# Graph attention on one Trainium2 core: messages and index copy moved within the slot of TensorE and VectorE

## The chip, the cores and the metric

The kernel runs on one core of one Trainium2 chip. The metric is device time in microseconds (us) of one execution. Three timed runs of the kernel before took 2605.95, 2622.97 and 2636.16 us; the median is 2622.97 us.

## What is computed

A graph of 1250 nodes with 768 features each and 41,250 directed edges goes through two layers of GATv2 attention, a linear-attention block and a feed-forward block. Only the attention layer matters here:

```
def gatv2_layer(x, Ws, bs, Wd, bd, attn, src, dst):
    hs = (x @ Ws + bs).reshape(N, H, HD)
    hd = (x @ Wd + bd).reshape(N, H, HD)
    hs_e = hs[src]
    e = jax.nn.leaky_relu(hs_e + hd[dst], SLOPE)
    logits = jnp.einsum('ehd,hd->eh', e, attn)
    m = jax.ops.segment_max(logits, dst, num_segments=N)
    ex = jnp.exp(logits - m[dst])
    s = jax.ops.segment_sum(ex, dst, num_segments=N)
    alpha = ex / s[dst]
    out = jax.ops.segment_sum(alpha[..., None] * hs_e, dst, num_segments=N)
    return jax.nn.elu(out).reshape(N, DM)
```

N is 1250, H is 8 heads of 96 features, and there are two such layers. The edges are sorted by destination.

## The kernel before

Before `attend` runs, `hs` of all nodes lies in HBM as `table` (1280 rows of 800 floats, 1250 of them nodes) and `hd` lies in SBUF as `dst_rows`. `attend` then walks over the edges in macros of 4 tiles of 128 edges (`G` = 4), 91 macros in each layer (`NM` = 91), 182 in both.

One macro goes through three steps, which belong to three different slots of the loop:

1. Turn. GpSimd has gathered the macro's 512 rows of `table` into `rows[b]` with four indirect DMAs of 128 rows (`gather`, L475 to L484), each by a column of `index[b]`. TensorE adds the destination's row and the gathered row in PSUM and turns them so that features lie on partitions (`turn_chunk`, L552): six chunks of 128 features, each with four pairs of matmuls (L559 and L561, one pair for each tile). ScalarE takes each chunk through a Relu into `at_relu` (`bend`, L502).
2. Head. VectorE joins the chunks of two pairs (`join`, L653). TensorE sums over the features of each head (`sum_heads`, L574 and L578, four tiles of 8 columns side by side). VectorE runs a scan from the left and one from the right for the segment maximum (`scan_left` L659, `scan_right` L664), subtracts it (`shift`, L668), TensorE turns the result back (`turn_back`, L584), ScalarE takes the exponential (`weights`, L512), and VectorE multiplies it into a one-hot matrix (`spread_out`, L676).
3. Message. TensorE multiplies this matrix with the gathered rows (`messages`, L597, 32 matmuls of which the trace shows two passes each, 64 in all; each uses 32 columns of the array). VectorE adds the totals to `sums` (`add_total`, L686, 8 instructions). After that the gathered rows are no longer needed, and VectorE copies the indices of the macro four later into the same buffer (`copy_index`, L696).

A slot works on three macros at once: head of h, message of h-1, turn of h+1. The engines run one slot function each, and the order inside it is written by hand. On TensorE (L601) it is: load of the block numbers (`places_of`), messages, chunk 0, heads, chunks 1 to 3, turn back, chunk 4, drops, linear part, chunk 5. On VectorE (L698): line up, join, additions, index copy, both scans, shift, first maximum, place, linear, spread. The four buffers of `rows`, `index` and `place` go round by macro number (`UNROLL` = 4).

The waits around the change are semaphores. GpSimd waits for `index_ready` before the four gathers of a macro; its third gather also waits for the counter `scanned` of three macros earlier to be complete (this counter's last step is `first_maximum`), and its fourth for `spread_ready`. Chunk 0 waits for `gathered[b]`, all 64 increments of the macro's four gathers, and for `place_ready`. The sending of the gathers, in its own words:

```
def gather(m, b, paced=True):
    pool.wait_ge(index_ready, m + 1)
    for j in range(G):
        if paced and j == 2:
            pool.wait_ge(scanned, (m - 3) * SCANS + 2 * SCANS)
        if paced and j == 3:
            pool.wait_ge(spread_ready, m - 2)
        pool.sem_inc(index_seen, 1)
        pool.indirect_dma_start(rows[b][:, j, :], None, table, ...)
```

So the macro whose index is copied in the slot of head h is h+3, and its chunk 0 stands in the slot of head h+2: two slots later.

## Time and profile before

| | |
|---|---|
| median of three runs | 2622.97 us |
| span of the profiled execution, first to last instruction | 2250.3 us |
| difference, outside the span | 372.7 us |
| busy share of the span: TensorE, VectorE, ScalarE, GpSimd | 96%, 75%, 50%, 40% |
| granted TensorE clock, mean | 0.986 |

The profile holds one execution, whose own time outside the span is not listed; the span is what the sums below are made against, and what lies around it (372.7 us against the median) is taken to stay. The two attention layers fill the stretches from about 539 to 1222 us and from about 1430 to 2120 us of the span, 61% of it. In a timeline row the columns are: start (us), duration (us), engine, line, operation, what is written and read, count; in brackets the idle time before it and what ended it. Merged rows give the time from the first start to the last end.

### The profile page before, as it was taken

Reading aid. Unit: us, or ns where it says so; the run is one execution under the profiler, and the core shown is the slowest. Engines: PE = TensorE matmul, PEld = TensorE weight load, DVE = VectorE, ACT = ScalarE, POOL = GpSimd, SP = SyncE. Lnnn points to the kernel's source line nnn. Section 1 sums busy time; section 2 is a strip of 40 time slices with the busy share of each in tenths; the row PEclk is TensorE's granted clock in tenths of the full one; section 3 lists DMA queues with packets and bytes.
Section 4 is the critical chain, followed back from the end, with each engine's and each line's share of the span. In section 5 each row is a group of like instructions: output and inputs, shape, how many; then the busy total and the mean of one; then the engine's idle time right before and its main releaser. Section 6 shows DMA issues by size and latency. Waiting matters only on the chain. (4 is left out here: it accounts for less than half of the span.)

```text
span 2250.3 us, 86767 instructions
## 1 busy us (share of the span) xinstructions
PE 2154.9 (96%) x31007; PEld 1684.2 (75%) x31007; DVE 1678.2 (75%) x4435; ACT 1133.4 (50%) x2749; POOL 896.5 (40%) x849
## 2 busy tenths in 40 slices
PE   8999999998999999999997999899999999999798
PEld 4665555555888888888886655688888888888676
DVE  5546872344888888888887755588888888888884
ACT  1101200034666666666664314566666666666584
POOL 0000001022666566666652211466656656656121
PEclk9999999999999999999998999999999999999899
DMA  5002044144777777787774024587777777777421
GB/s 192 1 0 71 20 142 133 57 131 133 249 250 247 249 250 243 248 252 239 247 245 153 29 97 132 168 252 242 251 242 248 240 245 250 244 246 238 171 88 48
DMA packets 143398, 404.07 MB, mean 180 GB/s; under 512 B 21811, under 2 KB 81625, under 8 KB 143073
## 3 DMA queue, kind: packets, MB, share of 16 engines
q0 software_dynamic: 59584, 298.64, 41.0%
q1 hardware_dynamic: 79691, 93.00, 13.8%
q10 hardware_dynamic: 3828, 7.85, 1.0%
q8 instruction: 264, 4.33, 0.8%
q14 instruction: 31, 0.25, 0.0%
HBM read 370.77 MB, written 17.17 MB: 172 GB/s over the span
## 5 line engine op out<-in xcount | busy, mean ns | idle before, releaser
L502 ACT ACTIVATE at_relu<-at_turned,ah_attn_size 128x512 f32<-128x512 f32 x1092 | 716.2, 692 | 392.0 <-PE at_heads L578 363.4
L483 POOL DMA_INDIRECT at_rows<-table,ah_index x360 | 404.6, 1124 | 269.0 <-DVE ah_index L696 158.5
L483 POOL DMA_INDIRECT ah_room<-table,ah_index x352 | 399.8, 1136 | 260.8 <-DVE ah_index L696 174.3
L561 PE MATMUL at_turned<-ident,ah_room 128*128 128x128 f32 x2208 | 427.9, 280 | 2.3 <-issue 2.3
L559 PE MATMUL at_turned<-ah_place,dst_rows 96*128 96x128 bf16 x2208 | 407.7, 223 | 23.4 <-ACTq L537 19.2
L561 PE MATMUL at_turned<-ident,at_rows 128*128 128x128 f32 x2160 | 413.3, 277 | 1.7 <-issue 1.4
L559 PE MATMUL at_turned<-at_place,dst_rows 96*128 96x128 bf16 x2160 | 394.1, 222 | 2.2 <-issue 1.5
L686 DVE SCALAR_TENSOR_TENSOR sums<-sums,at_factor,at_total 128x97 f32 x1456 | 343.7, 310 | 1.4 <-DVE at_gap L751 0.7
L561 PEld LDWEIGHTS at_turned<-ident,ah_room 128*128 128x128 f32 x2208 | 318.1, 144 | 26.2 <-issue 1.7
L561 PEld LDWEIGHTS at_turned<-ident,at_rows 128*128 128x128 f32 x2160 | 307.8, 143 | 24.5 <-issue 2.2
L676 DVE TENSOR_TENSOR at_spread<-at_lined,at_weight 128x1024 f32<-128x1024 f32 x182 | 223.3, 1227 | 127.7 <-ACT at_weight L512 127.7
L559 PEld LDWEIGHTS at_turned<-ah_place,dst_rows 96*128 x2208 | 224.1, 103 | 60.6 <-issue 60.5
L653 DVE SCALAR_TENSOR_TENSOR at_relu<-at_relu,ah_pair_sign 128x512 f32<-128x512 f32 x364 | 256.3, 746 | 0.0
L559 PEld LDWEIGHTS at_turned<-at_place,dst_rows 96*128 x2160 | 217.4, 103 | 36.8 <-issue 36.6
L597 PE MATMUL at_total<-at_rows,at_spread 128*32 128x100 f32 x5760 | 144.3, 253 | 1.9 <-DVE at_spread L676 1.8
L597 PE MATMUL at_total<-ah_room,at_spread 128*32 128x100 f32 x5888 | 145.7, 251 | 0.3 <-issue 0.2
L597 PEld LDWEIGHTS at_total<-ah_room,at_spread 128*32 128x32 f32 x5888 | 125.6, 110 | 12.3 <-DVE at_spread L676 2.4
L597 PEld LDWEIGHTS at_total<-at_rows,at_spread 128*32 128x32 f32 x5760 | 124.5, 111 | 13.2 <-DVE at_spread L676 3.9
L518 ACT ACTIVATE at_factor<-at_back,first_dst 128x2 f32<-128x2 f32 x728 | 132.8, 283 | 1.1 <-PE at_back L589 1.1
L578 PE MATMUL at_heads<-at_relu,ah_sign_mask 128*8 128x128 f32 x2912 | 116.5, 273 | 1.6 <-issue 1.4
L574 PE MATMUL at_heads<-at_relu,ah_sign_mask 128*8 128x128 f32 x2912 | 114.0, 273 | 0.2 <-issue 0.2
L1748 ACT ACTIVATE pr_parts<-pr_dst_row 128x384 bf16<-128x384 f32 x60 | 31.2, 522 | 124.9 <-DVEq L1845 112.0
(317 smaller groups left out, 3179.7 us busy)
## 6 DMA issues: line engine op xcount, KB each, us to landing
at_flags<-run_flags SPq DMA_DIRECT2D x182, 64.0 KB
dst_rows<-pr_parts SPq DMA_DIRECT2D x76, 144.0 KB, 2.6
ah_place<-local_rows SPq DMA_DIRECT2D x92, 96.0 KB
at_place<-local_rows SPq DMA_DIRECT2D x90, 96.0 KB
table<-ah_room SPq DMA_DIRECT2D x20, 400.0 KB, 2.4
ah_room<-table,ah_index POOLq DMA_INDIRECT x368
at_rows<-table,ah_index POOLq DMA_INDIRECT x360
mx_w<-in_L_mix_W_qkv SPq DMA_DIRECT2D x4, 1152.0 KB, 11.8
```

The costliest lines, as they stand in the source:

```text
L483: pool.indirect_dma_start(rows[b][:, j, :], None, table, bass.IndirectOffsetOnAxis(index[b][:, j:j + 1], 0)).then_inc(gathered[b], 16)
L502: act.activation(relu[c][:], turned[chunk(b, c)][:], ACT.Relu, scale=attn_size[:, c:c + 1]).then_inc(bent, 1)
L518: act.activation(factor[b % 2][:, j, :], back[:, P + j * HH:P + (j + 1) * HH], ACT.Exp, scale=first_dst[:, bass.ds(m * G + j, 1)]).then_in ...
L559: pe.matmul(into, dst_rows[0:SP_ROWS, bass.ds(at[j], 1), c * P:(c + 1) * P].rearrange("p o d -> p (o d)"), place[b][:, j * P:(j + 1) * P], ...
L561: last = pe.matmul(into, rows[b][:, j, c * P:(c + 1) * P], ident[:], is_transpose=True, start=False, stop=True)
L574: pe.matmul(head_row(j), sign_mask[:, c, :], relu[c][:, j * P:(j + 1) * P], start=False, stop=False)
L578: last = pe.matmul(head_row(j), sign_mask[:, c, :], relu[c][:, j * P:(j + 1) * P], start=False, stop=c == JOINED[-1][1])
L597: last = pe.matmul(part(j)[h % HM * S:(h % HM + 1) * S, h // HM, :], spread[:, j, h, :], rows[b][:, j, :].rearrange("p (g h r) -> p h g r" ...
L653: dve.scalar_tensor_tensor(relu[c][:], relu[from_][:], pair_sign[:, c:c + 1], relu[c][:], ALU.mult, ALU.add).then_inc(joined, 1)
L676: dve.tensor_tensor(spread[:], lined[:].unsqueeze(2).broadcast_to([P, G, H, S]), weight[:].rearrange("p (j h) -> p j h", j=G).unsqueeze(3) ...
L686: dve.scalar_tensor_tensor(into[:, k], into[:, k], factor[b % 2][:, j, k:k + 1], part(j)[:, k, 0:HW], ALU.mult, ALU.add).then_inc(added, 1)
L1748: act.activation(heads_half(parts[t % 2][:, s, :], half), heads_half(dst_row[:], half), ACT.Copy).then_inc(split_done, 1)
```

## The change

TensorE's slot now begins with chunks 0 and 1, then sums the heads, then does the messages; chunk 2, the turn back, and chunks 3 and 4 follow. The block numbers of the next slot are loaded (`blocks(coming)`) after the messages of this one, in place of a load at the slot's start. VectorE builds the place matrix and the linear part right behind the joins, runs the scans and the shift, then waits for the messages (`totalled`), copies the index, and only then does the eight additions, the first maximum and the spread. Nothing is added to or taken from the arithmetic.

```
--- before.py
+++ after.py
@@ -598,39 +598,42 @@
                                              rows[b][:, j, :].rearrange("p (g h r) -> p h g r", h=H, r=QUAD)[:, h], start=True, stop=True)
                     last.then_inc(totalled, 1)
 
-                def slot(turn, head, message):
+                def blocks(turn):
+                    return places_of(nc, mybir.EngineType.PE, block_of, turn[0], 1) if turn else None
+
+                def slot(turn, head, message, at, coming):
                     if turn:
-                        at = places_of(nc, mybir.EngineType.PE, block_of, turn[0], 1)
+                        turn_chunk(*turn, at, 0)
+                        turn_chunk(*turn, at, 1)
+                    if head:
+                        sum_heads(head[0], head[1])
                     if message:
                         for pair in range(2):
                             messages(message[0], message[1], pair)
+                    after = blocks(coming)
                     if turn:
-                        turn_chunk(*turn, at, 0)
-                    if head:
-                        sum_heads(head[0], head[1])
-                    if turn:
-                        for c in range(1, 4):
-                            turn_chunk(*turn, at, c)
+                        turn_chunk(*turn, at, 2)
                     if head:
                         turn_back(head[0])
                     if turn:
+                        turn_chunk(*turn, at, 3)
                         turn_chunk(*turn, at, 4)
                     if head:
                         sum_drops(head[0])
                     if turn:
                         turn_linear(turn[0])
                         turn_chunk(*turn, at, 5)
+                    return after
 
                 pe.sem_inc(weights_ready, EXPS)
                 pe.sem_inc(added, ADDS)
-                slot(macro(0, 0), None, None)
-                slot(macro(0, 1), macro(0, 0), None)
-                for i in range(LOOPS):
-                    for b in range(UNROLL):
-                        slot(macro(i, b + 2), macro(i, b + 1), macro(i, b))
-                slot(macro(LOOPS, 2), macro(LOOPS, 1), macro(LOOPS, 0))
-                slot(None, macro(LOOPS, 2), macro(LOOPS, 1))
-                slot(None, None, macro(LOOPS, 2))
+                at = blocks(macro(0, 0))
+                at = slot(macro(0, 0), None, None, at, macro(0, 1))
+                at = slot(macro(0, 1), macro(0, 0), None, at, macro(0, 2))
+                for m in range(2, NM):
+                    at = slot(macro(0, m), macro(0, m - 1), macro(0, m - 2), at, macro(0, m + 1) if m + 1 < NM else None)
+                slot(None, macro(0, NM - 1), macro(0, NM - 2), None, None)
+                slot(None, None, macro(0, NM - 1), None, None)
                 pe.wait_ge(merge_ready, 1)
                 pe.wait_ge(weights_ready, NM * EXPS + EXPS)
                 pe.matmul(back[:, 0:2 * G * HH], head_rows[:], gap[:].rearrange("p s k -> p (s k)"), start=True, stop=True).then_inc(merged, 1)
@@ -701,21 +704,22 @@
                     if head:
                         line_up(head[0], fresh)
                         join(head[0])
-                    if message:
-                        for j in range(G):
-                            add_total(message[0], message[1], j, at)
-                    if more:
-                        copy_index(message[0] + UNROLL, message[1])
-                    if head:
-                        scan_left(*head)
-                        scan_right(head[0], head[1])
-                        shift(head[0])
-                        first_maximum(head[0])
                     if after:
                         build_place(*after)
                     if turn:
                         line_linear(*turn, head is None)
                     if head:
+                        scan_left(*head)
+                        scan_right(head[0], head[1])
+                        shift(head[0])
+                    if more:
+                        dve.wait_ge(totalled, message[0] * 2 + 2)
+                        copy_index(message[0] + UNROLL, message[1])
+                    if message:
+                        for j in range(G):
+                            add_total(message[0], message[1], j, at)
+                    if head:
+                        first_maximum(head[0])
                         spread_out(head[0], head[1])
 
                 dve.memset(linear[:], 0.0).then_inc(cleared, 1)
```

TensorE before, around the start of a steady slot in the first layer (at_turned are the chunks' PSUM banks, at_total the messages', ISA rows compute an address from the block number):

```order
L559 MATMUL at_turned_0<-ah_place,dst_rows 128x128
L561 MATMUL at_turned_0<-ident,ah_room 128x128
L370 TENSOR_LOAD block_of
L597 MATMUL at_total_0<-ah_room,at_spread 32x100 x32
L559 ISA
L559 MATMUL at_turned_0<-at_place_0,dst_rows 128x128
L561 MATMUL at_turned_0<-ident,at_rows_0 128x128
L559 ISA
```

and around the head sums of the same slot (at_heads):

```order
L559 MATMUL at_turned_0<-at_place_0,dst_rows 128x128
L561 MATMUL at_turned_0<-ident,at_rows_0 128x128
L574 MATMUL at_heads<-at_relu_0,ah_sign_mask 8x128 x8
L578 MATMUL at_heads<-at_relu_0,ah_sign_mask 8x128 x8
L559 ISA
L559 MATMUL at_turned_0<-at_place_0,dst_rows 128x128
```

TensorE after, the end of chunk 1 and what follows:

```order
L559 ISA
L559 MATMUL at_turned_0<-at_place_0,dst_rows 128x128
L561 MATMUL at_turned_0<-ident,at_rows_0 128x128
L574 MATMUL at_heads<-at_relu_0,ah_sign_mask 8x128 x8
L578 MATMUL at_heads<-at_relu_0,ah_sign_mask 8x128 x8
L597 MATMUL at_total_0<-ah_room,at_spread 32x100 x32
L370 TENSOR_LOAD block_of
L559 ISA
L559 MATMUL at_turned_0<-at_place_0,dst_rows 128x128
L561 MATMUL at_turned_0<-ident,at_rows_0 128x128
```

The head sums and the messages stand next to each other, the load of block numbers has moved behind them, and the messages no longer come first.

VectorE before, in the loop of the second layer, the last additions of a slot and what follows (sums are the totals, at_left and at_right the two scans):

```order
L686 ISA
L686 SCALAR_TENSOR_TENSOR sums<-sums,at_factor_1,at_total_1 128x97
L686 ISA
L686 SCALAR_TENSOR_TENSOR sums<-sums,at_factor_1,at_total_1 128x97
L696 ISA
L696 COPY ah_index<-src_index 128x4
L659 SCALAR_TENSOR_TENSOR at_left_1<-at_flags_1,at_left_1,at_heads 128x128
L663 REGISTER_ALU
L664 SCALAR_TENSOR_TENSOR at_right<-at_flags_1,at_left_1 128x128
L667 REGISTER_ALU
L668 TENSOR_TENSOR at_shifted<-at_heads,at_right 128x128
```

VectorE after, from the left scan on (L716 is the new wait's instruction):

```order
L662 SCALAR_TENSOR_TENSOR at_left_1<-at_flags_1,at_left_1,at_heads 128x128
L666 REGISTER_ALU
L667 SCALAR_TENSOR_TENSOR at_right<-at_flags_1,at_left_1 128x128
L670 REGISTER_ALU
L671 TENSOR_TENSOR at_shifted<-at_heads,at_right 128x128
L716 ISA
L699 ISA
L699 COPY ah_index<-src_index 128x4
L683 REGISTER_ALU
L685 REGISTER_ALU
L686 ISA
L689 ISA
```

The index copy stood behind the additions and ahead of the scans; now both scans and the shift stand ahead of it, and the additions behind it.

## Rows read from the trace of the kernel before

**Rows 1.** The page: TensorE's busy time, and DMA's busy tenths in 40 slices

```profile
PE 2154.9 (96%) x31007; PEld 1684.2 (75%) x31007; DVE 1678.2 (75%) x4435; ACT 1133.4 (50%) x2749; POOL 896.5 (40%) x849
...
DMA  5002044144777777787774024587777777777421
```

**Rows 2.** Windows, a steady stretch: busy us of each engine, clock, DMA share, GB/s

```profile
700.00:900.00 200.00, 199.02 (x4061) 174.53 (x4049) 175.65 (x516) 135.38 (x357) 122.71 (x110) 1.00 0.78 248
```

**Rows 3.** Waits, whole span: engine, line, what it waited for, total us, times, longest

```profile
ACT at_relu L502 <- PE at_heads L578: 363.4, 180, 3.1
...
POOL ah_room L483 <- DVE ah_index L696: 174.3, 88, 7.7
...
DVE at_spread L676 <- ACT at_weight L512: 127.7, 182, 2.1
```

**Rows 4.** Timeline of TensorE, one slot of the first layer: start, us, engine, line

```profile
861.82 0.28 PE L561 MATMUL at_turned<-ident,at_rows 128*128 128x128 f32 x1
...
862.03 1.58 PE L597 MATMUL at_total<-at_rows,at_spread 128*32 128x100 f32 x64
...
863.54 0.23 PE L559 MATMUL at_turned<-ah_place,dst_rows 96*128 96x128 bf16 x1
...
864.13 0.28 PE L561 MATMUL at_turned<-ident,ah_room 128*128 128x128 f32 x1
...
864.34 0.62 PE L574 MATMUL at_heads<-at_relu,ah_sign_mask 128*8 128x128 f32 x16
...
864.78 0.62 PE L578 MATMUL at_heads<-at_relu,ah_sign_mask 128*8 128x128 f32 x16
...
865.33 0.23 PE L559 MATMUL at_turned<-ah_place,dst_rows 96*128 96x128 bf16 x1
...
865.92 0.28 PE L561 MATMUL at_turned<-ident,ah_room 128*128 128x128 f32 x1
...
866.04 0.22 PE L559 MATMUL at_turned<-ah_place,dst_rows 96*128 96x128 bf16 x1
```

**Rows 5.** Timeline of TensorE at the first layer's end, where heads follow messages

```profile
1209.48 1.58 PE L597 MATMUL at_total<-ah_room,at_spread 128*32 128x100 f32 x64
...
1210.88 0.62 PE L574 MATMUL at_heads<-at_relu,ah_sign_mask 128*8 128x128 f32 x16
```

**Rows 6.** Timeline of VectorE: the spreads that bound the layer, and one slot

```profile
551.29 1.23 DVE L676 TENSOR_TENSOR at_spread<-at_lined,at_weight 128x1024 f32<-128x1024 f32 x1 [1.08 <-ACT at_weight L512]
...
860.69 1.23 DVE L676 TENSOR_TENSOR at_spread<-at_lined,at_weight 128x1024 f32<-128x1024 f32 x1 [0.65 <-ACT at_weight L512]
...
863.60 1.89 DVE L686 SCALAR_TENSOR_TENSOR sums<-sums,at_factor,at_total 128x97 f32 x8
865.40 0.17 DVE L696 COPY ah_index<-src_index 128x4 int32 x1
865.47 0.48 DVE L659 TENSOR_TENSOR_SCAN at_left<-at_flags,at_left,at_heads 128x128 f32<-128x128 bf16 x1
...
867.97 1.23 DVE L676 TENSOR_TENSOR at_spread<-at_lined,at_weight 128x1024 f32<-128x1024 f32 x1 [0.67 <-ACT at_weight L512]
...
1208.20 1.23 DVE L676 TENSOR_TENSOR at_spread<-at_lined,at_weight 128x1024 f32<-128x1024 f32 x1 [1.07 <-ACT at_weight L512]
```

**Rows 7.** Timeline of GpSimd: first and last gather of the macro indexed at 865.40

```profile
866.36 0.95 POOL L483 DMA_INDIRECT at_rows<-table,ah_index  x1 [1.86 <-DVE ah_index L696]
...
870.32 1.44 POOL L483 DMA_INDIRECT at_rows<-table,ah_index  x1 [0.30 <-issue]
```

**Rows 8.** Timeline of TensorE: chunk 0 of that same macro

```profile
878.18 0.23 PE L559 MATMUL at_turned<-at_place,dst_rows 96*128 96x128 bf16 x1
```

**Rows 9.** Timeline of GpSimd, the first layer's last macro of gathers

```profile
1191.78 0.94 POOL L483 DMA_INDIRECT at_rows<-table,ah_index  x1 [1.85 <-DVE ah_index L696]
...
1195.93 1.45 POOL L483 DMA_INDIRECT at_rows<-table,ah_index  x1 [0.30 <-issue]
```

**Rows 10.** Windows behind it: columns as in rows 2, DMA share and GB/s last

```profile
1199.00:1200.00 1.00, 1.00 (x14) 0.93 (x13) 0.97 (x5) 1.00 (x3) 0.00 (x0) 1.00 0.44 122
1200.00:1201.00 1.00, 1.00 (x14) 0.94 (x12) 0.25 (x3) 0.67 (x4) 0.00 (x0) 1.00 0.15 55
1201.00:1202.00 1.00, 1.00 (x14) 0.95 (x12) 1.00 (x1) 1.00 (x3) 0.00 (x0) 1.00 0.00 0
```

## The prediction, made before the changed kernel ran

> **What bounds the kernel now.** I read the page first. TensorE is busy 96% of the span, and in the attention layers every slice of the DMA row stands at 7 tenths [rows 1]. The windows view of a steady stretch says it more sharply: of 200 us TensorE is busy 199.02, VectorE 175.65, ScalarE 135.38, and the 16 DMA engines 0.78 of the time at 248 GB/s; the clock is granted in full [rows 2]. So TensorE's order of work sets the slot, and nobody waits long for anybody: the reader is to see in the waits that ScalarE waits for the heads (363.4 us), GpSimd for indices (174.3 us) and VectorE for the weights (127.7 us over 182 slots, 0.70 each), which cost nothing while TensorE is full [rows 3].
>
> The period of a quiet slot is the distance of two spreads, 867.97 - 860.69 = 7.28 us. Over the first layer it is (1208.20 - 551.29) / 89 = 7.38 us [rows 6]; the 0.10 between are odd stalls. There are 180 such steps in two layers, 1,330 us of the span.
>
> TensorE is busy, but not dense. A full-width matmul group followed by another starts 0.16 us before the nominal end of the one ahead: 865.92 + 0.28 against 866.04. Where it changes from full width to narrow columns or back, the next starts only 0.07 before the end: 861.82 + 0.28 against 862.03 (chunk to messages), 863.61 against 863.54 (messages to chunk), 864.13 + 0.28 against 864.34 (chunk to heads), 865.40 against 865.33 (heads to chunk) [rows 4]. Messages and heads are both narrow, and at the layer's end, where heads follow messages, they start 0.18 before the end (1211.06 against 1210.88) [rows 5]. So each change of width costs about 0.10 us, and a slot has four of them. The page "TensorEngine Tiling (Array Packing)" of the Trainium skill, section Key Properties, gives the mechanism: a change of tiling mode drains TensorE, a change of tile within a mode does not. By that rule alone the change would be faster.
>
> **The change on TensorE.** The orders show chunk, heads, messages, chunk. Two changes of width go (chunk to messages, heads to chunk), and in their place come chunk 5 to chunk 0 and heads to messages, neither of them a change of width. That takes off 2 x 0.10 = 0.20 us: a quiet slot would be 7.08 us. All matmuls stay. The load of block numbers moves behind the messages; the trace's rows do not count such instructions, so I bound it: nothing if TensorE has enough queued, and at most the 0.35 us of idle time that would show in front of chunk 2 if all of it came bare. That end is my estimate from the whole gain and a little more; behind 64 narrow matmuls (1.58 us [rows 4]), which the sequencer can hand over ahead of time, I take 0.
>
> **The change on VectorE and ScalarE.** The scans come as soon as the heads are there, as before (865.40 to 865.47, [rows 4, 6]), so ScalarE gets its work at the same point. The additions (1.80 us, 863.60 to 865.40) move behind the shift, into the 0.70 us of waiting for the weights and beyond it. VectorE's work stays at 175.65 / 200 x 7.28 = 6.39 us of a slot [rows 2], under 7.08. I cost both at 0.
>
> **The change on GpSimd's gathers.** This is the step that decides. GpSimd can gather macro h+3 only when VectorE has copied its index, and TensorE wants its rows in chunk 0, two slots later. Both ends of this lead move against each other. Let T be the end of the heads of slot h.
>
> Before: the index is copied at T (865.40, where the heads end at 864.78 + 0.62), the first gather issues 0.96 later at 866.36, and chunk 0 of that macro starts at 878.18 [rows 4, 6 to 8]. From first issue to use there are 11.82 us, and chunk 0 shows no wait.
>
> After: chunk 0 starts earlier in its slot, for it now comes first. From its start to the end of the heads it is 0.80 (863.54 to 864.34) for a chunk with its change of width, 1.06 (864.34 to 865.40) for the heads, and 0.70 for chunk 1, in all 2.56 us [rows 4]. And the copy comes later: the messages start 0.18 before T and take 1.58, so they end at T + 1.40, and the copy waits for them, with 0.07 from signal to start as before the scan: T + 1.47. The first issue is at T + 1.47 + 0.96 = T + 2.43. Chunk 0 wants the rows at T + 2P - 2.56, P being the slot. At P = 7.08 that leaves 14.16 - 2.56 - 2.43 = 9.17 us from issue to use, where before there were 11.82.
>
> How long do the four gathers need from first issue to the last landing? No row shows a wait for them, so I bound it. Below: the first layer's last gathers issue from 1191.78 on, the last starts at 1195.93, and data still move from 1200 to 1201 (0.15 of the engines, 55 GB/s) and none after [rows 9, 10]: 9.0 us to the end of the data, with no macro behind it. Above: 11.8, as chunk 0 does not wait. The signal comes after the last byte, and in the steady stretch the next macro's gathers share the engines; nearest to the row of 9.0, I take 10.0.
>
> The page "DMA: Bandwidth & Descriptors" of the Trainium skill, section Anatomy of one DMA, puts a gather-like transfer at a fixed 2.0 us plus its bytes over 436 GB/s; by that a gather of 128 rows x 3200 B needs an estimated 2.9 us, the last lands 4.1 + 2.9 = 7.1 us after the first issue, and no one waits. The trace disagrees: data alone moved for longer than that [rows 10]. The same section says that most of the fixed part is the receipt after the last byte, which goes with a landing later than 9.0.
>
> With 10.0, and 0.10 from landing to chunk 0, the lead closes only if 2P = 2.56 + 2.43 + 10.0 + 0.10 = 15.09, P = 7.55 us. This is above 7.08, so the gathers become the bound and TensorE waits 0.47 us ahead of each chunk 0. The gathers' pacing doesn't add to it: the third, due at T + 4.9, waits for the first maximum, which comes after the additions at about T + 1.54 + 1.80 = T + 3.4, and the fourth, due at T + 6.4 (3.96 after the first, [rows 7]), for the spread, which ends near T + 3.5 + 1.23 = T + 4.8.
>
> **The sum.** The odd stalls (0.10 a slot) lie partly behind the messages, where the new wait covers them; I keep 0.05. 7.55 + 0.05 = 7.60 against 7.38: +0.22 us a slot, x 180 = +40 us on the span, 2250.3 to about 2290. What lies around the span stays, so the median goes from 2622.97 to 2663.
>
> **The bounds** come from the landing alone. At 9.0 us P = 7.05, and TensorE's 7.08 holds: (7.08 + 0.10 - 7.38) x 180 = -36. At 11.8 P = 8.45: +200 us, for which nothing speaks, since a transfer that took that long would have shown chunk 0 waiting in the slower slots. Between 9.6 and 10.6 P goes from 7.35 to 7.85, the time from 2627 to 2717.
>
> **Rivals.**
> 1. *The gathers land in time, and the drains count: faster.* For it: 9.0 us to the end of the data in the last macro, just under the 9.17 left. Against it: the signal still has to come, and the steady stretch has traffic behind each macro. It holds if first issue to landing is under 9.2. Time: 2623 - 36 = 2587. The drain rule of the tiling page would give the same.
> 2. *VectorE's joins become late.* After the copy at T + 1.47 come additions to T + 3.4, spread to T + 4.8, line up and joins (about 0.25 and 1.41) to T + 6.5. The second half of the last head sums, 0.4 us before the heads' end, needs the second join: P = 6.5 + 0.05 + 0.4 = 6.95, or 7.17 if all the joined sums (0.62 [rows 4]) were behind it. It decides only where the gathers don't. Time between 2587 and 2603.
> 3. *The gathers pile up: clearly slower.* DMA is at 0.78 [rows 2]. If landings vary by 1 us, each slot waits for the late one and two neighbouring macros hinder each other: 11.0 us gives P = 8.05, +0.67 x 180 = +120: 2743. Against it: a longer slot gives DMA more room.
>
> **Chances.** The forecast, gathers as the bound by 0.1 to 0.8 us a slot, 0.70, its own range 2625 to 2710; rivals 1 and 2 together 0.20; rival 3 0.10. A measurement of this kernel tells about 1% (26 us) from no change. Of the forecast's 0.70 I count 0.52 as slower by more than 1%, 0.18 within it; of rivals 1 and 2, 0.15 faster and 0.05 within. So faster 0.15, same 0.23, slower 0.62. The range goes from 2587 to 2720, which leaves out most of rival 3 and the lower half of rival 1.
>
> **What would show it.** In the profile after: a row of waits of TensorE at chunk 0 (L559) with some 0.3 to 0.6 us in most of 180 slots; TensorE's busy share in a steady stretch at 0.93 or so, where now it is 0.995; the timeline of TensorE with heads and messages 0.18 us into each other; spreads 7.5 to 7.6 us apart; VectorE's waits for the weights gone, and VectorE waiting for the heads instead; GpSimd's first gather 2.4 us after the heads' end. Wrong, I would see no wait at chunk 0 and spreads 7.1 us apart. If chunk 0 waits but the slot is not longer than 7.3, the landing was mis-sized. If an idle stretch stands in front of chunk 2, it is the load of block numbers.

## The result, and the profile after

The changed kernel took 2761.67 us (2759.29 to 2761.91, 4 runs), the kernel before beside it 2625.81 us (2605.95 to 2636.16): ratio 1.0523, 95% interval 1.0479 to 1.0566. The prediction said 2663 us and 2587 to 2720. It was right that the change costs time, and wrong in the size and in the reason: the loss is 136 us, not 40. As the reason was wrong, the right direction is luck.

The page after, TensorE's row and DMA's, and two rows of the costliest groups:

```profile
PE 2284.6 (83%) x31007; PEld 1750.5 (63%) x31007; DVE 1699.7 (62%) x4435; ACT 1177.7 (43%) x2749; POOL 853.5 (31%) x849
...
DMA  4002433455555555555652244565555555555341
...
L502 ACT ACTIVATE at_relu<-at_turned,ah_attn_size 128x512 f32<-128x512 f32 x1092 | 715.9, 686 | 691.0 <-remote 259.2
...
L574 PE MATMUL at_heads<-at_relu,ah_sign_mask 128*8 128x128 f32 x2912 | 229.5, 291 | 376.1 <-ACT at_relu L502 259.1
```

Where [rows 1] had TensorE at 96%, it stands at 83%, and the row of the DMA engines went from 7 tenths to 5. Everything is thinner; no engine became the bound by being full. The windows view of the same steady stretch as [rows 2], then six short windows of one slot:

```profile
700.00:900.00 200.00, 156.56 (x2887) 131.53 (x2889) 127.67 (x368) 101.09 (x254) 83.63 (x78) 0.96 0.59 181
...
1006.00:1007.00 1.00, 1.00 (x15) 0.93 (x13) 0.86 (x3) 0.67 (x1) 0.69 (x2) 1.00 0.65 262
...
1008.00:1009.00 1.00, 0.40 (x2) 0.09 (x1) 0.52 (x2) 0.24 (x2) 1.00 (x1) 1.00 0.91 333
1009.00:1010.00 1.00, 0.14 (x1) 0.00 (x0) 0.19 (x1) 0.31 (x1) 0.08 (x1) 0.94 0.98 378
1010.00:1011.00 1.00, 0.57 (x12) 0.43 (x16) 0.00 (x0) 0.37 (x1) 0.00 (x0) 0.50 0.84 243
...
1012.00:1013.00 1.00, 1.00 (x32) 1.00 (x28) 0.93 (x3) 0.95 (x2) 0.00 (x0) 0.50 0.15 46
1013.00:1014.00 1.00, 1.00 (x41) 0.85 (x34) 0.22 (x1) 0.80 (x3) 0.00 (x0) 0.85 0.00 0
```

From 1008 to 1010 TensorE, VectorE and ScalarE are idle for the most part, and then the granted clock stands at 0.50, TensorE's lower level of 1.2 GHz. TensorE is idle for some 2.1 us in the slots that keep the full clock too; the clock fell in 44 of 180. Who waits for whom? The waits of the whole span:

```profile
PEld at_heads L574 <- ACT at_relu L502: 357.2, 199, 2.9
DVE at_left L662 <- PE at_heads L578: 289.8, 182, 3.4
ACT at_relu L502 <- remote: 259.2, 168, 5.0
...
DVE at_linear L696 <- remote: 194.4, 168, 1.2
...
PEld at_turned L559 <- issue: 58.0, 185, 10.3
```

VectorE's wait for the weights [rows 3] is gone, as forecast. But chunk 0 (L559) has no wait for a gather at all: the last line is all that its weight loads lose, to "issue". Instead the heads wait for ScalarE's Relu, and ScalarE waits 259.2 us for "remote", a releaser that the profile cannot name. The timelines of that slot show when these waits end. TensorE, chunk 5's last matmul, chunk 1's last, and the heads:

```profile
1005.74 0.28 PE L561 MATMUL at_turned<-ident,ah_room 128*128 128x128 f32 x1
...
1007.13 0.28 PE L561 MATMUL at_turned<-ident,at_rows 128*128 128x128 f32 x1
1007.34 0.40 PE L574 MATMUL at_heads<-at_relu,ah_sign_mask 128*8 128x128 f32 x6
1008.12 0.27 PE L574 MATMUL at_heads<-at_relu,ah_sign_mask 128*8 128x128 f32 x1 [0.39 <-issue]
1008.87 0.27 PE L574 MATMUL at_heads<-at_relu,ah_sign_mask 128*8 128x128 f32 x1 [0.47 <-issue]
1010.43 0.61 PE L574 MATMUL at_heads<-at_relu,ah_sign_mask 128*8 128x128 f32 x8 [1.29 <-ACT at_relu L502]
```

ScalarE, GpSimd and VectorE in the same slot:

```profile
1007.51 0.72 ACT L518 ACTIVATE at_factor<-at_back,first_dst 128x2 f32<-128x2 f32 x4 [0.85 <-remote]
1009.69 0.69 ACT L502 ACTIVATE at_relu<-at_turned,ah_attn_size 128x512 f32<-128x512 f32 x1 [1.45 <-remote]
```

```profile
1003.89 0.94 POOL L483 DMA_INDIRECT at_rows<-table,ah_index  x1 [4.74 <-DVE ah_index L699]
1005.14 0.95 POOL L483 DMA_INDIRECT at_rows<-table,ah_index  x1 [0.30 <-issue]
1006.40 0.95 POOL L483 DMA_INDIRECT at_rows<-table,ah_index  x1 [0.31 <-issue]
1007.65 1.44 POOL L483 DMA_INDIRECT at_rows<-table,ah_index  x1 [0.30 <-issue]
```

```profile
1009.69 0.19 DVE L696 COPY at_linear<-at_rows 128x32 f32<-128x32 f32 x1 [1.16 <-remote]
```

Chunk 5's last matmul is over at 1005.74 + 0.28 = 1006.02, but its Relu starts at 1009.69, 3.7 us later, in the same instant as VectorE's wait on TensorE ends. The trace's record of the semaphore increments agrees: chunk 5, chunk 0 and chunk 1 end at 1006.02, 1006.71 and 1007.40, and their three increments come at 1009.66, 1009.76 and 1009.85, after GpSimd's fourth gather has been issued (1007.65 + 1.44 = 1009.09). I call these completions held. TensorE's ends in the profile are modelled, not measured. The Trainium skill, "Perfetto Trace Analysis", section Tensor Engine Instruction (MATMUL, LD_WEIGHTS), says the same and adds that the semaphore goes out only when PSUM has acknowledged the write. So it is open whether the signal or the write behind it is late; the engines that wait see no difference.

Over the whole changed kernel, of the groups of matmuls (chunks, heads, messages) whose last matmul ends 1.0 to 1.5 us and 2.0 to 4.0 us after a macro's first gather issue, 97 to 100% are completed late by 1.6 to 3.5 us on average; of those that end 7 to 12 us after it, none.

### The profile page after: what moved, and what is told of

Its sections match the earlier page's. It is cut to its first block and busy times, and to the rows that moved or that the text cites. A ratio compares the mean times of both kernels' runs of the same rounds, so it can differ in the third digit from the quotient of the medians.

```text
span 2759.5 us, 86679 instructions
## 1 busy us (share of the span) xinstructions
PE 2284.6 (83%) x31007; PEld 1750.5 (63%) x31007; DVE 1699.7 (62%) x4435; ACT 1177.7 (43%) x2749; POOL 853.5 (31%) x849
## 3 DMA queue, kind: packets, MB, share of 16 engines
q0 software_dynamic: 59584, 298.64, 35.2%
## 5 line engine op out<-in xcount | busy, mean ns | idle before, releaser
L502 ACT ACTIVATE at_relu<-at_turned,ah_attn_size 128x512 f32<-128x512 f32 x1092 | 715.9, 686 | 691.0 <-remote 259.2
L483 POOL DMA_INDIRECT ah_room<-table,ah_index x352 | 377.5, 1073 | 565.7 <-DVE ah_index L699 481.6
L483 POOL DMA_INDIRECT at_rows<-table,ah_index x360 | 382.8, 1063 | 512.2 <-DVE ah_index L699 408.0
L559 PE MATMUL at_turned<-ah_place,dst_rows 96*128 96x128 bf16 x2208 | 406.9, 224 | 28.4 <-ACTq L537 19.3
L559 PE MATMUL at_turned<-at_place,dst_rows 96*128 96x128 bf16 x2160 | 391.3, 222 | 0.0
L574 PEld LDWEIGHTS at_heads<-at_relu,ah_sign_mask 128*8 128x8 f32 x2912 | 62.9, 87 | 505.0 <-ACT at_relu L502 357.2
L662 DVE TENSOR_TENSOR_SCAN at_left<-at_flags,at_left,at_heads 128x128 f32<-128x128 bf16 x182 | 87.3, 480 | 289.8 <-PE at_heads L578 289.8
L559 PEld LDWEIGHTS at_turned<-ah_place,dst_rows 96*128 x2208 | 228.4, 104 | 44.4 <-issue 44.4
L559 PEld LDWEIGHTS at_turned<-at_place,dst_rows 96*128 x2160 | 220.7, 103 | 13.6 <-issue 13.6
L597 PE MATMUL at_total<-ah_room,at_spread 128*32 128x100 f32 x5888 | 172.8, 277 | 2.2 <-issue 2.2
L597 PEld LDWEIGHTS at_total<-ah_room,at_spread 128*32 128x32 f32 x5888 | 163.7, 127 | 6.3 <-issue 3.5
L597 PE MATMUL at_total<-at_rows,at_spread 128*32 128x100 f32 x5760 | 154.9, 260 | 8.3 <-issue 4.4
L597 PEld LDWEIGHTS at_total<-at_rows,at_spread 128*32 128x32 f32 x5760 | 141.9, 116 | 12.1 <-issue 6.9
```

Of the source, the lines that this page charges most:

```text
L483: pool.indirect_dma_start(rows[b][:, j, :], None, table, bass.IndirectOffsetOnAxis(index[b][:, j:j + 1], 0)).then_inc(gathered[b], 16)
L502: act.activation(relu[c][:], turned[chunk(b, c)][:], ACT.Relu, scale=attn_size[:, c:c + 1]).then_inc(bent, 1)
L559: pe.matmul(into, dst_rows[0:SP_ROWS, bass.ds(at[j], 1), c * P:(c + 1) * P].rearrange("p o d -> p (o d)"), place[b][:, j * P:(j + 1) * P], ...
L574: pe.matmul(head_row(j), sign_mask[:, c, :], relu[c][:, j * P:(j + 1) * P], start=False, stop=False)
L597: last = pe.matmul(part(j)[h % HM * S:(h % HM + 1) * S, h // HM, :], spread[:, j, h, :], rows[b][:, j, :].rearrange("p (g h r) -> p h g r" ...
L662: dve.tensor_tensor_scan(left[b % 2][:], flags[b][:, 0, :], heads[:, 0:P], left[(b + 1) % 2][:, P - 1:P], ALU.add, ALU.max).then_inc(scann ...
```

## The experiments

For each kernel I give the median time, and from its profile the mean slot (mean distance of two spreads within a layer, 180 of them) and in how many of these slots the granted clock was below full. The kernels without all of their gathers, with small gathers or with short additions leave out or replace part of the work, and each of them ran once.

| kernel | time us | mean slot | slots at lower clock |
|---|---|---|---|
| before, its first profile | span 2250.3 | 7.39 | 0 |
| before_again | 2633.8 | 9.36 | 18 |
| changed | 2761.67 | 10.14 | 44 |
| pe_only | 2805.3 | 10.35 | 79 |
| dve_only | 3086.4 | 11.93 | 141 |
| before_no_gather | 2246.1 | 7.28 | 0 |
| after_no_gather | 2263.4 | 7.39 | 0 |
| no_gather_short_adds | 2202.1 | 7.03 | 0 |
| after_two_gathers | 2318.5 | 7.69 | 0 |
| after_copy_late | 2641.6 | 9.48 | 21 |
| before_spaced | 2596.9 | 9.26 | 5 |
| after_pairs | 2628.4 | 9.40 | 0 |
| before_pairs | 2925.1 | 11.07 | 158 |

**The kernel before, once more.** No edit.

> The kernel before, unchanged, profiled once more. Its first profile has a span of 2250 us, while its runs took 2606 to 2636 us; of the changed kernel the profiled execution's span (2759.5) and its time (2761.6) agree. Theory 1, the first profile was of an execution in which the attention slots ran smoothly, which the timed ones don't: a second profile shows a span near 2620 and slots of about 9.3 us. Theory 2, some 370 us lie outside the span in every execution of this kernel: the span is near 2250 again, slots 7.28 us.

2633.8 us, ratio 1.0007 (0.9971 to 1.0043). The profiled execution took 2619.12 us with a span of 2617.4: only 1.7 us lie outside the span. Its steady stretch, and two of its waits:

```profile
700.00:900.00 200.00, 171.52 (x3114) 143.90 (x3112) 138.14 (x400) 106.58 (x274) 91.56 (x84) 0.97 0.63 191
```

```profile
DVE at_spread L676 <- ACT at_weight L512: 311.3, 177, 3.5
...
PE at_back L589 <- ACT at_weight L512: 148.6, 162, 2.6
```

TensorE is busy 171.52 of 200 us, not 199.02 as in [rows 2]. So the profile that the prediction was read from showed an execution of 2250 us that no timed run shows. This second profile, whose time agrees with the timed runs, has slots of 9.4 us, completions held already, and 311.3 us of waiting for the weights instead of 127.7. In the first profile no completion in the layers' slots is over 0.2 us late.

**Each half of the change alone.** pe_only has the new order on TensorE and the old one on VectorE; dve_only the reverse.

```
pe_only:  slot() of TensorE as changed;  slot() of VectorE as before
dve_only: slot() of TensorE as before;   slot() of VectorE as changed
```

> Only TensorE's order is the new one, VectorE's is the old one (additions and index copy ahead of the scans). Theory A, TensorE's new order costs the time, because chunk 5, chunk 0 and chunk 1 stand directly ahead of the head sums, which wait for ScalarE's Relu of chunk 5, and the signal of chunk 5 comes 3.6 us late in the changed kernel: about 2760 us or more, chunk 5's signal late again. Theory B, the gathers' lead costs it: the lead is shortened by TensorE's part only if the index is copied late; here the index copy comes after the additions, some 1.8 us later than in the changed kernel, so chunk 0 waits for gathers and it takes over 2800. Theory C, VectorE's new order costs it: about 2620.

> Only VectorE's order is the new one, TensorE's is the old one. Theory A (TensorE's new order costs the time): at most 2640 us, no more than the kernel before. Theory B (gathers' lead): the index is copied about 1 us later than before and chunk 0 stays behind the messages, so the same as before, 2620. Theory C (VectorE's new order): about 2760.

pe_only: 2805.3 us, ratio 1.0679 (1.0621 to 1.0737). dve_only: 3086.38 us, ratio 1.1745 (1.1674 to 1.1817). Each half alone is slower than the whole. dve_only is outside all three theories. pe_only has the time that theories A and B named, but the sign of neither: chunk 0 waits for no gather, and chunk 5 is completed late in 17% of the slots only, against 93% in the changed kernel. Its waits show another loss:

```profile
DVE sums L689 <- PE at_total L597: 626.1, 180, 5.2
...
PE at_back L584 <- DVE at_first_max L674: 388.7, 182, 2.7
```

TensorE now does the messages behind the heads, but VectorE still wants them ahead of its scans. So the additions wait for the messages, 3.5 us a slot, and TensorE's turn back waits for the scans behind them. How much of the 175 us is this and how much comes from the gathers, no run separates.

In dve_only the gathers fall just ahead of chunk 5's end, and its Relu waits even longer than in the changed kernel. GpSimd's and ScalarE's timelines, and TensorE's:

```profile
1004.19 0.94 POOL L483 DMA_INDIRECT ah_room<-table,ah_index  x1 [7.03 <-DVE ah_index L696]
...
1007.94 1.46 POOL L483 DMA_INDIRECT ah_room<-table,ah_index  x1 [0.30 <-issue]
```

```profile
1010.00 0.69 ACT L502 ACTIVATE at_relu<-at_turned,ah_attn_size 128x512 f32<-128x512 f32 x1 [3.17 <-remote]
```

```profile
1005.65 0.28 PE L561 MATMUL at_turned<-ident,at_rows 128*128 128x128 f32 x1
1006.86 0.87 PE L597 MATMUL at_total<-ah_room,at_spread 128*32 128x100 f32 x26 [0.94 <-DVE at_spread L676]
1008.52 0.26 PE L597 MATMUL at_total<-ah_room,at_spread 128*32 128x100 f32 x1 [0.79 <-issue]
1009.25 0.36 PE L597 MATMUL at_total<-ah_room,at_spread 128*32 128x100 f32 x3 [0.47 <-issue]
```

Chunk 5 ends at 1005.93 and ScalarE takes it at 1010.00. The messages too, which wait for nothing that the profile shows, come to single matmuls 0.73 us apart: in the same stretch TensorE itself goes slower. The record of increments is complete here for chunks, heads and messages, so all of them can be sorted: of those whose matmul ended 1.0 to 6.0 us after the first gather issue 95 to 100% were late, of the others 0 to 2%.

**The load of the block numbers** back at the slot's start:

```
 def slot(turn, head, message, at, coming):
+    at = blocks(turn)
...
-    after = blocks(coming)
```

> The changed kernel, but with the load of the slot's block numbers at the slot's start, between chunk 5 and chunk 0, and none behind the messages. Theory A, a late signal of the last chunks when they run straight into the head sums: a pause of 0.3 us in TensorE's instruction stream behind chunk 5 changes when its signal comes, so the slot gets shorter by up to the 3.6 us of lateness, or not at all if the wait of the head sums holds the signals: then within 1% of 2760. Theory L, the load behind the messages costs time ahead of chunk 2: faster than 2760 by up to 0.35 us x 180 = 60 us.

2762.14 us, ratio 1.0509 (1.0454 to 1.0564): its place is worth nothing, as costed.

**No gathers in the steady stretch.** The gathers of all macros behind the first four of a layer, and the waits for their landing, are left out, so the rows of later macros are those of the first ones.

```
 pool.sem_inc(index_seen, 1)
+if paced:
+    continue
...
-return 16 * G * (layer * len(range(b, NM, UNROLL)) + rounds)
+return 16 * G * (layer + 1)
```

> The kernel before, without the gathers of macros 4 to 90 of each layer (their rows stay those of macros 0 to 3) and without their landing waits. The second profile of the kernel before has slots of 9.3 us where its matmuls need 7.28, and TensorE's signals (turned_done, turned_back, totalled) come 0.7 to 2.3 us after the matmul's end while GpSimd's gathers are being issued. Theory G, the gathers hold TensorE's signals up: without them slots of 7.1 to 7.3 us, about 2250 us in all. Theory T, TensorE's stream itself stalls (its own code or its waits), whatever the gathers do: 2600 or more.

> The changed kernel, without the gathers of macros 4 to 90 of each layer and their landing waits. Theory G (gathers hold TensorE's signals up, and the changed order has more steps that wait on such a signal): the drains saved come out, slots of 7.05 to 7.15 us, 2210 to 2230 us in all, faster than the kernel before without gathers by some 36 us. Theory T (TensorE's stream stalls by itself in the new order): 2700 or more. My prediction's lead of the gathers would also vanish here, but it can't be told from theory G by this run alone: for that the next run.

2246.1 and 2263.4 us, where before took 2628.62 beside them. In the slots the clock is full. The second is outside the 2210 to 2230 us that I expected. So the gathers cost the kernel before 382 us and the changed one 498 us, and without them the change costs 17. The wait that the changed kernel then shows is the ring of rival 2:

```profile
PEld at_heads L580 <- DVE at_relu L658: 81.5, 179, 0.5
```

**Small gathers.** Each paced gather fetches 80 floats for a row, 320 B, instead of 800; the rest of the row is that of an earlier macro. The index now counts pieces of 320 B, so the pieces come from the first tenth of the table and are not the row's own.

```
+if paced:
+    pool.indirect_dma_start(rows[b][:, j, 0:80], None, table.rearrange("r (a c) -> (r a) c", c=80), ...)
+    continue
```

> The changed kernel, whose gathers of macros 4 to 90 move 320 bytes a row instead of 3200 (the other columns stay those of macros 0 to 3): as many gathers, issued at the same times, with a tenth of the bytes. Theory G1, it is GpSimd's issuing that holds TensorE's signals up: slots of 9.9 us as before, about 2760. Theory G2, it is the moving of the data (DMA busy, HBM and SBUF traffic): slots near 7.1, below 2300 us. The lead of the gathers as I predicted it would fall with G2 too, but the profile tells: landings ahead of chunk 0 by over 3 us in the changed kernel.

> The kernel before, gathers of 320 bytes a row instead of 3200. Theory G1 (issuing): slots of 9.3 us, about 2620. Theory G2 (data): slots of 7.3 us, about 2250.

2761.04 and 2640.8 us: a tenth of the data, the same time within 0.5%. GpSimd's queue also moved 26,176 packets instead of 59,584 in the changed kernel. So the amount of data doesn't matter; what is left is the issuing itself, or the number of rows, which the edit keeps. For the issuing speaks the time: in the slot above, the held completions came 0.6 us after the fourth issue had ended, while the data moved on to 1013.

**Two gathers of four.**

```
-for j in range(G):
+for j in range(2 if paced else G):
```

> The changed kernel, but in the steady stretch GpSimd issues two of its four gathers a macro; the rows of the other two tiles stay those of an earlier macro, so part of the gathered rows is left out. Theory (GpSimd's issuing holds TensorE's signals back while the gathers behind the first are issued): with four gathers a slot is 9.9 us, with none 7.39. With two the stretch in which signals are held ends after the second gather, some 2.5 us earlier, so a slot should be 7.6 to 8.6 us and the time 2300 to 2480 us. Rival (a loss that comes with any gather in the slot, whatever their number): the slot stays above 9.5 us and the time above 2690 us.

2318.49 us, slot 7.69, within what the theory of held completions had forecast. GpSimd's and ScalarE's timelines:

```profile
1002.82 0.95 POOL L483 DMA_INDIRECT ah_room<-table,ah_index  x1 [5.45 <-DVE ah_index L699]
1004.08 0.95 POOL L483 DMA_INDIRECT ah_room<-table,ah_index  x1 [0.30 <-issue]
```

```profile
1004.89 0.69 ACT L502 ACTIVATE at_relu<-at_turned,ah_attn_size 128x512 f32<-128x512 f32 x1 [0.90 <-PE at_turned L561]
```

A chunk that ends beside the first gather is completed at once; chunk 4, which ends at 1003.97, beside the start of the second, waits until 1004.89. The held stretch is short, other work covers it, and it costs 0.30 us a slot against 2.75 with four.

**The index copy back behind the additions**, one part of the change undone:

```
-    dve.wait_ge(totalled, message[0] * 2 + 2)
-    copy_index(message[0] + UNROLL, message[1])
 if message:
     for j in range(G):
         add_total(message[0], message[1], j, at)
+if more:
+    copy_index(message[0] + UNROLL, message[1])
```

> The changed kernel with one part undone: the index copy stands behind the additions again, some 1.9 us later in the slot, and with it GpSimd's gathers. Theory (held signals): the four gathers are issued as before, so the loss per slot stays of the order of 2.5 us, but it falls on other work: chunk 5 would be signalled in time and the held signals would be those of chunks 0 and 1, of the heads and of the messages. I expect a time that moves by more than 1% either way, 2680 to 2850 us, and late signals again only from 1.0 to 6.0 us after the first issue. Rival (the place of the copy matters only through the landing of the rows, which are 3 us early): within 0.5% of the changed kernel, 2750 to 2775 us.

2641.63 us, ratio 1.0057 (1.0032 to 1.0083): below the 2680 us that I expected from the held completions, and far from the rival, to which the place of the copy meant nothing. This one edit takes back 120 of the 136 us. GpSimd's timeline, then TensorE's:

```profile
1005.02 1.28 POOL L483 DMA_INDIRECT at_rows<-table,ah_index  x1 [3.77 <-DVE ah_index L699]
1006.61 1.45 POOL L483 DMA_INDIRECT at_rows<-table,ah_index  x1 [0.30 <-issue]
1008.36 0.95 POOL L483 DMA_INDIRECT at_rows<-table,ah_index  x1 [0.30 <-issue]
1009.61 0.94 POOL L483 DMA_INDIRECT at_rows<-table,ah_index  x1 [0.30 <-issue]
```

```profile
1009.11 0.62 PE L578 MATMUL at_heads<-at_relu,ah_sign_mask 128*8 128x128 f32 x16
1009.55 0.51 PE L597 MATMUL at_total<-at_rows,at_spread 128*32 128x100 f32 x12
1010.36 0.39 PE L597 MATMUL at_total<-at_rows,at_spread 128*32 128x100 f32 x6 [0.29 <-issue]
```

Every chunk is now completed in time (in 95% of the slots within 0.1 us). What is held is the heads, which end at 1009.73 while VectorE's scan starts at 1011.22, and, in 42% of the cases, the messages. The idle of TensorE became shorter, and the clock fell in 21 slots instead of 44.

Two things differ from the changed kernel, and this run does not part them. First, the copy is later, so the chunks end sooner after the first issue: chunk 5 some 0.8 us after it in 163 of 174 macros, where it was 2.1 us. (The slot shown is one of the other 11.) Second, the hold itself begins later. In the changed kernel the first late completion ends 1.1 us after the first issue, here 3.3 us (medians). In the slot shown chunk 5 ends 2.33 us after the first issue, beside the second gather, and is in time all the same, where in the changed kernel 2.13 us meant 3.6 us of lateness. So the position of the work against the burst is not the whole account.

**The gathers of before spaced one by one.**

```
-if paced and j == 2:
+if paced and j == 1:
     pool.wait_ge(scanned, (m - 3) * SCANS + 2 * SCANS)
-if paced and j == 3:
+if paced and j == 2:
     pool.wait_ge(spread_ready, m - 2)
+if paced and j == 3:
+    pool.wait_ge(joined, (m - 2) * 2 + 1)
```

> The kernel before with GpSimd's gathers of one macro spaced: the second waits for the scans of the chunk maxima, the third for the spread, the fourth for the joins of the next slot, where before two go at once and the others follow 1.3 us apart. Theory A (signals are held only while a gather is issued on the heels of another): with gaps between them the signals come out between two gathers, the slot falls from 9.33 us towards 7.3 and the time to 2250 to 2500 us. Theory B (each gather behind the first holds signals for its own 1.3 us wherever it stands): the held stretches are shorter but more, 2500 to 2700 us. Rival (what holds the signals is the amount of gathering in a slot, not its pacing): within 1% of before.

2596.87 us, ratio 0.9872 (0.9816 to 0.9928): the slot went from 9.36 to 9.26 only. Theory A falls. The time lies in theory B's range, but so does that of the kernel before, and the interval reaches into the rival's 1%: this run does not decide between those two.

**No gathers, short additions.** On top of after_no_gather, the eight additions touch one column, so the sum of the messages is left out.

```
-dve.scalar_tensor_tensor(into[:, k], into[:, k], factor[...], part(j)[:, k, 0:HW],
+dve.scalar_tensor_tensor(into[:, k, HD:HW], into[:, k, HD:HW], factor[...], part(j)[:, k, HD:HW],
```

> The changed kernel without its paced gathers (the rows of later macros are left out) and with the eight additions of a slot on the column of the denominators alone (the sum of the messages is left out). Without gathers the changed kernel had slots of 7.39 us, and the heads waited for VectorE's joins (81.5 us in 179 waits). Theory (ring from the heads through scans, additions, first maximum, spread and joins back to the heads): the additions lie in the ring, so shorter ones open it, the heads no longer wait, and the two saved changes of width show: slot 7.05 to 7.15 us, time 2200 to 2220 us. Rival (heads are stretched by TensorE's own handling of heads behind chunks): the slot stays at 7.35 to 7.4 us, 2255 to 2265 us.

2202.09 us. TensorE's second half of the heads, in after_no_gather and in this kernel, one fence each:

```profile
1004.58 0.95 PE L580 MATMUL at_heads<-at_relu,ah_sign_mask 128*8 128x128 f32 x16
```

```profile
1004.53 0.62 PE L580 MATMUL at_heads<-at_relu,ah_sign_mask 128*8 128x128 f32 x16
```

The wait for the joins is gone and the slot is 7.03 us, against 7.28 of before_no_gather, whose additions are the long ones. There TensorE is busy throughout, so shorter additions would have nothing to give:

```profile
700.00:900.00 200.00, 199.94 (x4054) 176.07 (x4054) 174.32 (x526) 135.91 (x355) 0.00 (x0) 1.00 0.09 25
```

So the two saved changes of width are real, 0.25 us.

**Pairs of gathers**, in the changed kernel and in before:

```
 if paced and j == 2:
-    pool.wait_ge(scanned, (m - 3) * SCANS + 2 * SCANS)
-if paced and j == 3:
-    pool.wait_ge(spread_ready, m - 2)
+    pool.wait_ge(joined, (m - 2) * 2 + 1)
```

> The changed kernel, with all four gathers a macro, but in two pairs: the third waits for the first joined sums of the next slot, some 1.6 us after the second has been issued, and the fourth follows it at once. Theory A (what costs is a long burst, for the third and the fourth gather prolong one held stretch from 1.5 to 4 us, and a pair alone cost 0.25 us a slot): two pairs cost 0.5 us, slot 7.8 to 8.1 us, time 2340 to 2430 us. Theory B (a gather leaves TensorE's signals alone only after a pause of several us, whatever its place in a burst): four gathers hold for 1.0 to 1.5 us each, nearly all day, slot 9.0 to 9.9 us, time 2590 to 2770 us. What lies between, 2430 to 2590 us, would say that the length of a burst and the pause both count.

> The kernel before with its four gathers a macro in two pairs: the third waits for the first joined sums of the next slot, the fourth follows at once. Spaced one by one they gave a slot of 9.1 us against 9.33. Theory A (long bursts cost, pairs are nearly free): slot 7.6 to 8.1 us, time 2310 to 2410 us. Theory B (only a gather behind a pause of several us is free): slot 9.0 to 9.4 us, time 2570 to 2650 us. If after_pairs is the faster of the two, the order of the changed kernel is the better one once the held stretches are short.

after_pairs took 2628.38 us, before_pairs 2925.1, and the kernel before 2696.07 beside them (ratios 0.9760, 0.9733 to 0.9786, and 1.0855, 1.0823 to 1.0886). Both speak against theory A: pairs with a pause of 2.3 us (in after_pairs) do not cost as little as one pair alone. after_pairs lies in theory B's range; before_pairs is worse than both theories. There the second pair of one macro and the first of the next close up to one burst again, and it falls on the heads: a group that ends at 1000.67 is completed at 1004.86 by the record of increments. In after_pairs the steady stretch has the full clock:

```profile
700.00:900.00 200.00, 168.07 (x3122) 139.63 (x3119) 136.46 (x402) 106.61 (x276) 82.13 (x84) 1.00 0.68 193
```

**Pairs and changed kernel once more**, since before had moved:

> The changed kernel with its gathers in two pairs, once more. It took 2628 us where before took 2696 beside it, but before took 2624 to 2634 us beside every other kernel of this study. If 2696 was a matter of that chip for the kernel before alone, this run gives 2625 to 2635 us again and a ratio of 1.00 against before at 2625 to 2635, and the pairs only take back the loss of the change. If the ratio 0.976 holds, pairs take 2560 to 2580 us where before takes 2630, and the version beats both kernels.

> The changed kernel unchanged, beside the pairs and before. Theory (the pairs end the held stretch between the second and the third gather, so chunk 0 and 1 are signalled in time): after stays 4.5 to 5.5% above the pairs and above before, 2755 to 2765 us. Rival (after moves with the chip as before did): its ratio to before falls under 1.03 or rises over 1.07.

2627.82 and 2762.17 us, with before at 2687.49: ratios 0.9771 (0.9725 to 0.9817) and 1.0267 (1.0219 to 1.0315). By its letter the second ratio is the rival's mark (under 1.03), but the kernel that moved is before, not the changed one. Neither alternative for the pairs came true: their time stayed at 2628 and the ratio held, as before was slow again. The two changed kernels repeat to 1 us on the chips that they ran on; the kernel before took 2626 to 2634 us beside all earlier kernels and 2696 and 2687 on the chips of these last two comparisons. So the change costs 5.2% on the first and 2.7% on the last, and the paired version beats the kernel before by 2.3 to 2.4% where both ran on one chip, and is only level with its times on the others. It takes 4.9% less than the changed kernel (2627.82 against 2762.17) on one chip.

## Why the prediction was wrong, by its steps

**"What lies around the span stays."** This is the step that failed first. The prediction put 372.7 us outside the span and built on slots of 7.28 us with a full TensorE. Outside the span lie 2 us, and the slot of a timed run is 9.36 us. A span of 2250.3 beside runs of 2606 us and more was a sign that the profile showed another execution, and the prediction explained it away. With it the sum lost its largest term: it has none for held completions. They are why a slot with gathers takes 2.08 us more than one without in before, and 2.75 in the changed kernel. The difference, 0.67 us, and the 0.11 of the ring below are the 0.78 us by which the mean slot grew, 9.36 to 10.14.

**"This is the step that decides": the landing of the gathers.** It fell. Chunk 0 waits for no gather, and with a tenth of the data nothing changes. The lead was computed at 9.17 us, on a slot of 7.08 us and 2.56 us from chunk 0 to the heads' end. In the profile after it is 11.5 to 13.5 us, as the slot is 10.14 us and the hold stands between chunk 0 and the heads' end. The landing of 10.0 us was too long as well: no data moves from 1013 on, 9.1 us after the first issue at 1003.89. (The 9.0 us that it was built on can be read from [rows 9, 10] only as at most 9.2.) The step looked at the right instruction, the index copy, and gave it the wrong effect: what counts is not when the rows land but what TensorE completes in the 5 us in which the gathers are issued.

**"I cost both at 0": VectorE's order.** Mis-sized. Copying the index in front of the additions costs 120 us (after_copy_late). It moves the four issues earlier against TensorE's work, onto chunks 5, 0 and 1, whose Relus the heads directly behind them need. Behind the additions the burst meets the heads and messages, with other work to go on with, and the hold begins later in it (3.3 us after the first issue, not 1.1). That the copy costs the 120 us is shown; how they divide between these two is not.

**The sum of the loss.** In slots at full clock the slot went from 9.20 to 9.77 us, and the 44 slots at lower clock take 11.29, against 18 of 10.76. With only 18 such slots the changed kernel would need 162 x 9.77 + 18 x 11.29 = 1786 us in its layers, 102 more than the 162 x 9.20 + 18 x 10.76 = 1684 of before; the other 26 x (11.29 - 9.77) = 40 come with the clock. The two make 142 us, the difference of the two profiled spans (2759.5 and 2617.4). Of the 102, 17 are there without any gather.

**The two changes of width: right.** Predicted 0.20 us and 7.08; measured 0.25 and 7.03, where nothing else binds. This agrees with the rule of the Trainium skill that was named there, "TensorEngine Tiling (Array Packing)", section Key Properties, that a change of tiling mode drains TensorE. But what it gives never reaches the timed kernel.

**Rival 2: real, and undersized.** Forecast at 6.95 to 7.17 us; measured 7.39 without gathers. Its additions, spread and joins do close the ring, and it eats the whole gain of the drains and 0.11 us more. **Load of block numbers at 0:** right. **Signs:** VectorE's waits for the weights gone, VectorE waiting for the heads, heads and messages 0.18 us into each other, the first gather some 2.4 us after the heads' end (2.5 measured): seen; the wait at chunk 0, TensorE at 0.93 and spreads at 7.5: not seen.

**What stays open.** Why the first profile of before has the same bursts and no held slot, and why one chip gives 2687 where another gives 2630. Which resource the issuing takes from TensorE's completions, and whether the write or the signal is late, no run here tells. No rule by pause or place in the burst covers all of it either. The first gather of a burst held nothing in after_copy_late (1% of 161 completions, pause 3.5 us and more) nor in dve_only; between 1 and 3 us of pause the kernels differ. The second held nearly everything in the changed kernel, before_again and dve_only (97 to 99% of the completions beside it were late), but a third in after_copy_late and nothing in pe_only, whose third held 18% and whose fourth 89%.

## What to carry to other kernels

Compare the profiled span with the timed median before reading anything else; if they differ by 14%, the profile shows another execution, and no slot length from it may be used. Where GpSimd issues indirect DMAs in a burst, look in the trace at what TensorE finishes in the next microseconds and when it is completed, and put there work whose result nobody needs at once: moving one small copy was worth 120 us. Few issues a slot, or two bursts of two in the changed order, did more than any saved drain. And when an order is changed on two engines, try each half: each alone was slower than both here.

## What the hardware showed that I had not expected

- While GpSimd issues a burst of four indirect gathers, completions of TensorE's matmuls reach the other engines up to some 4 us late, and the waits view often names no more than "remote" for it. The first late one ends 1.1 us after the first issue in the changed kernel and 3.3 us in after_copy_late; in one profile of before none is late. It is independent of the bytes (320 B or 3200 B a row), and costs 2.1 us a slot in before (9.36 against 7.28) and 2.75 in the changed kernel.
- It grows faster than the count: two gathers 0.30 us, four 2.75.
- In the changed kernel, where a slot has some 2 us of idle TensorE, the granted clock fell to 0.50 in 44 of 180 slots, in the one shown from 1010 to 1013, and such slots took 11.3 us instead of 9.8.
